# Flamingo block on one core: four normalised queries moved behind the block border, the norm's power moved ahead of GpSimd's masking, the sixth query moved to the ramp's end

## The reference

```python
x = x + tanh(g_xattn[0]) * wkv(layernorm(x), ctx)             # recurrence over 128 tokens
x = x + tanh(g_ffn[0])   * glu(layernorm(x))                  # silu(x Wg) * (x Wu), then Wd
x = x + tanh(g_xattn[1]) * cross_attention(layernorm(x), ctx) # 16 heads of 8
x = x + tanh(g_ffn[1])   * (top-1 experts + shared expert)(layernorm(x))
```

```python
q = Wq @ layernorm(x)[b] + bq;  k = Wk @ ctx[b] + bk;  v = Wv @ ctx[b] + bv   # 128 x 256
dot = q k / sqrt(8) per head;  dot = mask * dot - (1 - mask) * 1e6
out = (softmax(dot) * mask) v
```

## Time and profile before

| | us |
|---|---|
| three runs | 509.32, 510.07, 510.05; median 510.05 |
| profiled execution, own time | 509.36 |
| its span in the trace | 507.6 |
| busy: PE 474.1, DVE 381.3, ACT 244.9, POOL 230.1 | |
| first block ends, second begins (PE) | about 125 and 125.87 |
| ramp's first gate group (L602) | 142.21 |
| attention loop's first scores (L1190, L1205) | 178.92 |

### The profile page before, as it was taken

How to read it: one execution, slowest core, us unless ns; L and a number is a source line. 1 busy time by engine, 2 the same in 40 slices (tenths; PEclk the granted TensorE clock), 3 DMA queues, 4 the chain that set the end, 5 groups by cost and what they waited for, 6 DMA issues and landing times. The chain is left out here.

```text
span 507.6 us, 10286 instructions
## 1 busy us (share of the span) xinstructions
PE 474.1 (93%) x3384; PEld 259.3 (51%) x3384; DVE 381.3 (75%) x765; ACT 244.9 (48%) x461; POOL 230.1 (45%) x319
## 2 busy tenths in 40 slices
PE   2998999998999999999999998998999999999993
PEld 2663664854733633343343333333445647788882
DVE  4989889899888789999999999998465633333321
ACT  2761232332232078889999998787412010233331
POOL 3736434154755355867677763213010660042433
PEclk9999999999999999999999999999999999999998
DMA  7750175002775116566566655300022224378843
GB/s 237 216 176 0 43 166 89 2 0 62 186 195 150 54 57 174 147 171 184 162 163 172 171 153 147 84 5 5 1 94 77 74 94 166 120 185 195 192 112 41
DMA packets 67256, 59.96 MB, mean 118 GB/s; under 512 B 10048, under 2 KB 62256, under 8 KB 67216
## 3 DMA queue, kind: packets, MB, share of 16 engines
q1 hardware_dynamic: 63712, 55.24, 39.6%
q0 software_dynamic: 3072, 4.21, 4.9%
q10 hardware_dynamic: 432, 0.00, 0.0%
HBM read 38.90 MB, written 22.50 MB: 121 GB/s over the span
## 5 line engine op out<-in xcount | busy, mean ns | idle before, releaser
L1325 DVE TENSOR_REDUCE MX<-psum 128x2 f32<-128x512 f32 x256 | 162.1, 682 | 10.0 <-PE psum L1190 8.4
L1374 ACT ACTIVATE HP<-psum 128x512 f32<-128x512 f32 x224 | 122.1, 602 | 28.9 <-PE psum L1205 26.4
L1190 PE MATMUL psum<-QKA 60*128 60x256 bf16 x512 | 81.3, 273 | 7.1 <-DVE MX L1325 5.6
L1205 PE MATMUL psum<-QKA 60*128 60x256 bf16 x512 | 81.1, 273 | 1.5 <-DMA QKA<-max_scr 1.0
L1291 PE MATMUL psum<-HP,VP 128*32 128x256 f32 x1024 | 81.8, 391 | 0.3 <-issue 0.2
L602 PE MATMUL psum<-space_a,space_w 128*128 128x512 f32 x160 | 73.1, 602 | 1.9 <-DVE HP L629 1.9
L1190 PEld LDWEIGHTS psum<-QKA 60*128 60x128 bf16 x512 | 31.6, 94 | 63.8 <-DVE MX L1325 44.6
L1966 POOL DMA_INDIRECT out_x<-OE,to_u x16 | 24.9, 1557 | 62.6 <-ACT OE L2001 60.1
L602 PEld LDWEIGHTS psum<-space_a,space_w 128*128 128x128 f32 x160 | 29.0, 190 | 36.5 <-issue 31.0
L2089 PE MATMUL psum<-XT,WE 128*128 128x256 f32 (+1 forms) x192 | 44.0, 379 | 0.9 <-ACT XT L1985 0.9
L199 PE MATMUL psum<-space_a,wsh 128*128 128x512 f32 (+1 forms) x96 | 43.6, 598 | 0.3 <-PEq L1497 0.3
(11 more groups left out here) (207 smaller groups left out, 767.3 us busy)
## 6 DMA issues: line engine op xcount, KB each, us to landing
QKA<-stack_scr SPq DMA_DIRECT2D x32, 480.0 KB, 4.5
stack_scr<-PARTS SPq DMA_DIRECT2D x32, 192.0 KB, 2.1
WE<-in_W SPq DMA_DIRECT2D x16, 352.0 KB, 4.0
stack_scr<-PARTS SPq DMA_DIRECT2D x32, 128.0 KB, 2.0
XD<-dispatched SPq DMA_DIRECT2D x8, 258.0 KB, 3.9
X<-in_x SPq DMA_DIRECT2D x4, 512.0 KB, 5.8
CTX<-in_ctx SPq DMA_DIRECT2D x4, 512.0 KB, 8.2
MB<-in_mask SPq DMA_DIRECT2D x16, 128.0 KB, 3.3
```

The source lines that it names most:

```text
L1190: return pe.matmul(to[:, tt * T:(tt + 1) * T], QKA[rows, k, 0, h, tt * P:(tt + 1) * P], QKA[rows, k, 1, h, :], start=True, stop=True)
L1205: return pe.matmul(to[:, (m % 2) * T:(m % 2 + 1) * T], QKA[rows, k, 1, h, st * P:(st + 1) * P], QKA[rows, k, 0, h, :], start=True, stop=True)
L1325: dve.tensor_reduce(MX[:, par, head_of(n), :], src[:, :].rearrange("p (a s) -> p a s", a=2), axis=AX.X, op=ALU.max).then_inc(a_red, 1)
L1374: act.activation(PT[:, i % 2, st, 2 * half:2 * half + 2, :].rearrange("p j t -> p (j t)"), TBK3[THIRDS[m]], ACT.Exp).then_inc(a_exp, 1)
```

## The change

What moves, engine by engine:

- DVE: Z3 of queries 1 and 2 leave the first block. Z3 of 1 now stands between the statistics and the Z2 of `dve_ln2(G3)`, that of 2 behind the Z2, that of 3 behind `dve_stats3(1)`, that of 4 behind `dve_stats3(2)`, and that of 5 (`AHEAD_Q`) behind the first X of group 3.
- PE: the projection of query 1 leaves the first block for the place where that of 2 stood; that of 2 goes behind the transposes; that of 4 into the ramp's first group; that of 5 behind the ramp.
- ACT: `act_zt` ahead of QK of query 2.
- POOL: the power for Z2 first in the block; the power for batches 4 to 7 ahead of `pool_clear`.

```diff
@@ layer_norm_steps
-        def layer_norm_steps(ch, src, dst, n, s_var, s_rstd, nth, s_tile):
+        def layer_norm_steps(ch, src, dst, n, s_var, s_rstd, nth, s_tile, between=None):
             layer_norm_stats(ch, src, n).then_inc(s_var, 1)
+            if between:
+                between()
             ch.eng.wait_ge(s_rstd, nth)
@@
-            QB = {2: bank[5], 3: bank[4]}
+            QB = {1: bank[5], 2: bank[4], 3: bank[5]}
@@ tensor, first block
-                            if i == 3 and g == NG - 2:
-                                pe.wait_ge(a_qk, 1)
-                                pe_proj_q(pe, 0, 1)
@@ vector, first block
                             if i == 1:
-                                if last:
-                                    dve_z3(dve, 1)
                                 dve_scan_a(dve, g + 1, 1)
...
-                            if i == 3 and last:
-                                dve_z3(dve, 2)
@@ scalar, second block
-                        act_qk(act, 1)
+                        act_qk(act, 1, QB[1])
                         act_part(act, 1, 0)
                         act_part(act, 1, 1)
+                        act_zt(act, G3)
                         act_qk(act, 2, QB[2])
-                        act_zt(act, G3)
@@ gpsimd, second block
+                        power_step(pool, GB, s_var2, s_rstd2, NG)
                         pool_query(pool, 0, 1)
-                        pool_rest(pool, 1, 0)
-                        power_step(pool, GB, s_var2, s_rstd2, NG)
-                        pool_rest(pool, 1, 1)
+                        for r in range(2):
+                            pool_rest(pool, 1, r)
                         pool_masked(pool, 0, 2)
+                        pool_power3(pool, 1)
                         pool_clear(0)
-                        pool_power3(pool, 1)
@@ tensor, second block
-                            if (b, p) == (1, 4):
-                                pe.wait_ge(a_nm, 1)
-                                pe_proj_q(pe, 1, 1)
...
-                        pe_down(pe, NG - 2, 0, DBW, None, lambda: pe.wait_ge(a_qk, 2))
-                        pe_proj_q(pe, 0, 2, QB[2])
-                        parts = [None, None, None, lambda: pe_z2T(pe, G3), None, None]
+                        pe_down(pe, NG - 2, 0, DBW, None, lambda: pe.wait_ge(a_qk, 1))
+                        pe.wait_ge(s_x1, 2 * NG)
+                        pe_proj_q(pe, 0, 1, QB[1])
+                        parts = [None, None, None, lambda: (pe_z2T(pe, G3), pe_proj_q(pe, 0, 2, QB[2])), None, None]
...
                         pe_down(pe, NG - 2, 1, DBW, turn_z2)
+                        pe.wait_ge(a_qk, 2)
                         pe_proj_q(pe, 0, 3, QB[3])
                         pe_gu(pe, G3, 0)
                         pe.wait_ge(s_x2, 1 + 2 * G3)
-                        pe_proj_q(pe, 1, 0)
                         pe.wait_ge(a_qk, 4)
                         for i in range(1, NI):
                             for side in range(2):
                                 pe_gu(pe, G3, i, (side,))
                                 pair()
+                                if i == 1 and side == 1:
+                                    pe_proj_q(pe, 1, 0)
                         pe_down_by_tiles(pe, G3, DB, pair)
                         while pairs:
                             pair()
                         pe.wait_ge(a_red, 2 * HEADS)
+                        pe.wait_ge(a_nm, 1)
+                        pe_proj_q(pe, 1, 1)
@@ vector, second block
-                        dve_ln2(dve, fch, G3)
+                        dve_ln2(dve, fch, G3, lambda: dve_z3(dve, 1))
+                        dve_z3(dve, 2)
+                        dve_stats3(dve, ln3, 1)
                         dve_z3(dve, 3)
-                        dve_stats3(dve, ln3, 1)
                         dve_x2(dve, NG - 2, DBW)
+                        dve_stats3(dve, ln3, 2)
                         dve_z3(dve, GB)
-                        dve_stats3(dve, ln3, 2)
...
-                            if i == 4:
-                                dve_z3(dve, AHEAD_Q)
                         reduces(1, 4, 16)
                         dve_x2(dve, G3, DB, (0,))
                         dve.wait_ge(s_x2, 1 + 2 * G3 + 1)
+                        dve_z3(dve, AHEAD_Q)
```

More of the change, by code:

```diff
@@ L548, in act_z1, with dve_ln2 @@
                 last.then_inc(s_z1, 1)
-            def dve_ln2(dve, ch, g):
+            def dve_ln2(dve, ch, g, between=None):
                 dve.wait_ge(s_x1, 2 * g + 2)
@@ L553, in dve_ln2 @@
                 alone(dve)
-                layer_norm_steps(ch, xt_tile(g), lambda i: Z2[:, i, :], GB, s_var2, s_rstd2, g + 1, s_z2)
+                layer_norm_steps(ch, xt_tile(g), lambda i: Z2[:, i, :], GB, s_var2, s_rstd2, g + 1, s_z2, between)
             def dve_ln2_first(dve, ch, between):
```

## The result

| | us |
|---|---|
| kernel before, six executions | 509.32 to 510.28, median 510.06 |
| changed kernel, six executions | 513.80 to 515.20, median 514.10 |
| ratio | 1.0086, 95% interval 1.0073 to 1.0099 |
| profiled execution of the changed kernel | 515.20, span 513.5 |

The change makes the kernel slower by 4.0 us by the medians, 4.4 us by the ratio (3.7 to 5.0). The forecast was 512.3 us, which is 2.2 us above the kernel before. The sign was right, the size a little over half. Three executions of the later sections (598.01 us of `filler_half`, 1567.70 us of `q1_back_bank7`, 914.17 us of the kernel before beside the last two runs) lie far above all others, and the ratios leave them out.

What follows compares the result with a forecast made beforehand. TensorE, busy 93% of the span, was taken as the bound. Terms 2.64 + 0.5 - 0.3 - 0.5 + 0.5 - 0.2 = +2.6 us on 509.7 gave 512.3 us, range 510.6 to 514.4.

Steps and rivals of the forecast that it cites:

- The border: End of the first block: with two Z3 gone from DVE, every engine leaves 0.82 us earlier, PE at 125.05.
- Z2: Behind the border: power ahead of the masking has Z2 done near 131, and PE's 0.37 us stop in the transposes goes.
- The chain: Queries' steps from projection to store: query 1 behind the border makes PE start gate group 1 2.64 us later.
- Query 4: Its projection moves into gate group 1 and costs +0.5 us there.
- query 5: Around the ramp: Z3 leaving DVE's maxima -0.3, projection -0.5 and +0.5, wait for DVE's last X -0.2 us.
- The start of the loop: Attention loop behind the ramp: first scores start near 181.5 us, before 178.9.
- The clock: Rival at the gap before gate group 1: PE's clock falls, 3.4 us more, +6.0 in all, 515.7 us; chance 0.08.
- The faster rival: QK of query 3 comes before PE ends gate group 0 (141.2 us); gains alone, -1.7 us, 508.0; chance 0.12.

Runs made afterwards that it cites:

- filler_half: The changed kernel with two matmuls of unused result in front of PE's wait for the fourth QK; median 513.69 us, ratio 1.0075.
- q1_back_bank7: The changed kernel with query 1 back in the first block, query 3 in bank 7 and ACT's tanh ahead of PARTS; 508.40 us, ratio 0.9978.
- the last two runs: The changed kernel with query 3 in bank 7 and third tanh ahead of PARTS, measured again (507.93 us), and q1_back_bank7 (508.40 us).
- four filler matmuls: The changed kernel with four matmuls of unused result in front of PE's wait for the fourth QK; 512.17 us, ratio 1.0056.
- q1_alone: The kernel before with only queries 1 and 2, and what moves with them, behind the border; 514.66 us, ratio 1.0097.
- q1_back: The changed kernel with query 1 normalised and projected in the first block and POOL's order as before; 512.04 us, ratio 1.0039.

## Why the prediction was right and wrong

**The border: right.** PE left it at 124.95; forecast 125.05. Gate group 4 started 0.93 us earlier than before (117.59 instead of 118.52), the last store in front of the border 0.92 (121.23 instead of 122.15); the forecast had 0.82 for both.

**Z2: right.** 1.39 us in all, transposes without a stop. The power was moved for this.

**The chain: right in its order, and 0.4 us short in one link.** Forecast and measured: QK 130.91 and 130.81, PARTS 132.23 and 132.12, second PARTS 134.12 and 134.01, store 136.07 and 136.38, landed 140.45 and 140.75, QK of query 3 at 144.29 and 144.66, gate group 1 at 144.82 and 145.25 (its first weight load; the first matmul is at 145.28). The link is second rest to store: 1.66 us (134.72 to 136.38) instead of 1.25. The kernel before had both: 1.25 from 140.40 to 141.65, and 1.65 for the store of query 1, issued at 131.69 behind this rest on POOL:

```profile
130.04 1.15 POOL L739 TENSOR_TENSOR PARTS<-QK,PARTS 128x512 bf16<-128x512 f32 x1
```

I had taken the smaller. What SP does in those 0.4 us stays open. The term was 2.64 and measured 3.07 (145.25 less 142.18).

**Query 4, query 5: right.** The projection of query 4 costs 0.54 us in its new place (152.62 to 153.16), forecast 0.5. DVE's wait fell from 0.79 to 0.53 us, forecast 0.3 less. The experiment with query 5 alone gave -0.7 (interval 0.2 to 1.1) against the forecast's -0.5.

**The start of the loop: wrong.** The first scores were to start near 181.5 and started at 185.47. Of this, 2.9 us is the clock: with four filler matmuls they start at 182.60. That is still 3.7 behind the 178.92 of before, but the first matmuls on the value buffer `VP` come only 2.8 later (182.56 before, 185.39 with the filler), and 2.8 is what the whole kernel keeps. That the sum of +2.6 met these +2.8 is in part luck: the chain cost 0.4 us more than its term, and where the loop begins some of it was made up.

**The clock: wrong, and this is the step that failed.** The prediction had the mechanism as a rival at 0.08, with the sentence that "a gap of 3.6 us should pass". It rested on one place of the trace, the end of the kernel, where the granted clock falls only some 5 us after PE's last matmul. That was one sample of a thing that varies: 4.8 us there (matmuls end at 499.46, 0.62 for 504 to 505). In the changed kernel's trace the clock fell about 3.4 us after the last matmul (141.09, and 0.75 for 144 to 145), in that of `q1_alone` about 2.6 us after it (141.73, and 0.65 for the same stretch). So the step from that one place to "a gap of 3.6 us should pass" does not hold, and the forecast put the clock at nothing. Its sum of +2.6 is near what the run with four filler matmuls measured (+2.8); the rest of the +4.0 to +4.4, some 1.5 us, is the clock. The rival's own price, 3.4 us, was too high: 2.9 in the profiled execution, about 1.6 in four others. It was read from the length of the first matmuls alone; the windows of the trace of before give a granted clock of 1.00 from 10 to 17 us, so the clock's own row does not show that slow stretch. With the clock's fall as a term, the forecast would have been 2.6 + 1.6, or 513.9 from the same base of 509.7.

**The faster rival: wrong in its condition, and its size fits by luck.** It needed a chain that PE does not wait for. Where the experiments made that so, the gains came to 1.6 us (509.44 to 507.80), and the rival had summed them to 1.7. But its sum left out query 1's projection, which PE now does behind the border: with the 0.5 us for it, its own terms give 1.2. And the experiments also gave query 3 another bank and ACT another order. No run has these two in the kernel before, so how much of the 1.6 us is theirs is not shown.

## What to carry to other kernels

Before a step is moved to a later place, follow it forward through each single buffer to the next engine that waits for something behind it: here a query that ACT took up 5 us later (130.81 instead of 125.76) came back 10 us on, as a wait for a store's landing, and then on the busiest engine. Ask what that wait protects: it stood for a PSUM bank, and another bank took the loss away and left the gains. And a gap on TensorE has two prices, its length and what the clock loses behind it; where a gap of some microseconds is forecast, the second belongs into the sum, not among the rivals.

## What had not been expected

- Whether a gap brings the clock down does not seem to be settled by its length. In the runs whose traced gaps were 2.15 and 2.4 us, three of five executions each were 1.5 to 1.6 us slower at a lower mean clock; in the one with 4.2 us, all six had the lower clock. That the gaps of the untraced executions are like the traced ones is assumed.
- The price varies too. In the changed kernel's trace the half rate lasted some 6.8 us (144.5 to 151.3), in that of `q1_back` some 3.4 us (144.6 to 148.0).
- The fall can come after PE is at work again. With query 1 back in the first block, PE stood still from 141.42 to 143.57, and the windows of that trace read:

```profile
143.00:144.00 1.00, 0.43 (x1) 0.30 (x2) 0.00 (x0) 1.00 (x2) 1.00 (x2) 1.00 0.08 26
144.00:145.00 1.00, 1.00 (x3) 0.47 (x2) 0.83 (x2) 0.00 (x1) 1.00 (x2) 0.78 1.15 346
```

- Matmuls with no use made the kernel 1.5 us faster by the ratios.
- In the changed kernel, where a Z3 on DVE and a rest on POOL met, DVE alone paid: 1.24 us instead of 0.41, while the rest, begun 0.06 us earlier, took its usual 1.16. In the same trace it also went the other way: POOL's mask at 113.31 took 1.71 us instead of 0.72, beside a scan that DVE had begun at 113.28.
